# Two score banks and three banks for turned rows; both shared experts split in a row by GpSimd in the last pair

## The reference, cut to what matters

```python
qh = (layernorm(x) @ Wq) by heads; kh, vh = (ctx @ Wk), (ctx @ Wv) by heads
attn = softmax(qh @ kh.T * HEAD_DIM ** -0.5)
x = x + tanh(g_xattn) * ((attn @ vh) @ Wo + bo)
h = layernorm(x)
gates = softmax(h @ router_w); the best two of 14, weights normed to 1
ffn(e) = silu((h * rsqrt(mean(h * h)) * rms_w[e]) @ w1[e]) @ w2[e]
x = x + tanh(g_ffn) * (sum of the two routed ffn, weighted, + both shared ffn)
```

## Time and profile before

| | |
|---|---|
| median of 3 runs | 1499.19 us (1499.08 to 1499.24) |
| profiled execution, own time | 1498.68 us |
| its span, first to last instruction | 1497.0 us, mean granted clock 0.995 |
| busy: TensorE matmuls | 1441.7 us (96%) |
| busy: VectorE | 1086.8 us (73%) |
| busy: ScalarE | 958.3 us (64%) |
| busy: GpSimd | 440.7 us (29%) |
| chain that ended last | TensorE 78%, VectorE 10%, issue 5%, ScalarE 5% |
| pairs 1 to 14 | about 92 to 984 us |
| last pair's steps and the end of the attention | about 984 to 1066 us |

### The profile page before, as it was taken

One profiled execution on the slowest core, in us unless ns is written; L12 is line 12 of the kernel. 1 busy time (PEld: TensorE's weight loads), 2 busy tenths in 40 slices (PEclk: granted clock), 3 DMA queues, 4 the chain that ended last, 5 costly groups with the idle time before them and its releaser, 6 DMA issues.

```text
span 1497.0 us, 32793 instructions
## 1 busy us (share of the span) xinstructions
PE 1441.7 (96%) x9774; PEld 1344.9 (90%) x9774; DVE 1086.8 (73%) x2626; ACT 958.3 (64%) x2413; POOL 440.7 (29%) x676
## 2 busy tenths in 40 slices
PE   6999999999999999999999999998899999999998
PEld 6899999999999999999999999997689988888888
DVE  4778788887878878778787888878668634444448
ACT  4777777777777777777777776775363335455452
POOL 1013132331313313133231323324300135555520
PEclk9999999999999999999999999999999999999999
DMA  4011311212121130311213211141022256653235
GB/s 122 6 30 36 112 73 47 76 49 105 47 80 71 54 104 15 113 71 47 85 40 109 75 47 72 53 153 64 27 99 113 74 180 222 246 203 120 78 121 217
DMA packets 55294, 136.93 MB, mean 91 GB/s; under 512 B 10480, under 2 KB 38144, under 8 KB 51648
## 3 DMA queue, kind: packets, MB, share of 16 engines
q1 hardware_dynamic: 48608, 118.01, 22.7%
q0 software_dynamic: 6624, 18.13, 3.8%
HBM read 86.69 MB, written 49.43 MB: 91 GB/s over the span
## 4 chain that ended last, share of the span: by engine, by line
PE 78%; DVE 10%; issue 5%; ACT 5%; DMA 0%; ACTq 0%; DVEq 0%; POOL 0%; SPq 0%; POOLq 0%
PE bank L531 14%; PE bank L530 14%; PE bank L532 14%; PE bank L588 8%; PE bank L1590 6%; PE bank L933 5%; PE bank L925 5%; PE bank L1610 4%; DVE pT_lo L753 3%; PE bank L1614 2%; PE bank L1600 2%; DVE nmax L770 2%; ACT prob L678 1%; ACT L717 1%; ACT pT_hi L689 1%
## 5 line engine op out<-in xcount | busy, mean ns | idle before, releaser
L678 ACT ACTIVATE prob<-bank,nmax 128x375 f32<-128x375 f32 x448 | 258.7, 577 | 189.1 <-DVE nmax L770 187.2
L770 DVE TENSOR_REDUCE nmax<-bank 128x1 f32<-128x375 f32 x448 | 241.1, 538 | 48.4 <-PE bank L532 47.8
L753 DVE TENSOR_TENSOR pT_lo<-bank,pT_hi 125x384 fp32r<-125x384 f32 x448 | 246.0, 549 | 32.5 <-ACT pT_hi L689 30.7
L588 PE MATMUL bank<-keep_ident,prob 128*125 128x128 f32 x1344 | 225.4, 276 | 25.2 <-DVE pT_lo L753 22.9
L588 PEld LDWEIGHTS bank<-keep_ident,prob 128*125 128x125 f32 x1344 | 198.6, 187 | 45.8 <-DVE pT_lo L753 20.9
L689 ACT CAST pT_hi<-bank 125x384 fp32r<-125x384 f32 x448 | 212.6, 475 | 2.5 <-PE bank L588 2.4
L530 PE MATMUL bank<-attend_wvo_hi,zT_hi 128*112 128x256 f32 x512 | 169.5, 331 | 0.0
L530 PE MATMUL bank<-pT_hi,kv_hi 125*128 125x448 f32 x384 | 152.7, 398 | 6.1 <-DVE zT_lo L753 6.1
L530 PE MATMUL bank<-attend_kvT_hi,qp_hi 128*128 128x376 f32 x448 | 150.3, 335 | 0.2 <-DVE attend_kvT_lo L753 0.2
L531 PE MATMUL bank<-attend_kvT_hi,qp_lo 128*128 128x376 f32 x448 | 150.1, 335 | 0.0
L532 PE MATMUL bank<-attend_kvT_lo,qp_hi 128*128 128x376 f32 x448 | 149.0, 333 | 0.0
(11 more groups left out here) (234 smaller groups left out, 3729.3 us busy)
## 6 DMA issues: line engine op xcount, KB each, us to landing
w_split<-we_split SPq DMA_DIRECT2D x14, 2048.0 KB, 6.8
keep_weights<-w_split SPq DMA_DIRECT2D x14, 2048.0 KB
we_in<-in_w SPq DMA_DIRECT2D x28, 512.0 KB, 5.8
keep_y_all<-y_rows SPq DMA_DIRECT2D x14, 512.0 KB, 9.7
kv_in<-in_ctx SPq DMA_DIRECT2D x32, 187.5 KB
h_rows<-hrow SPq DMA_DIRECT2D x32, 112.4 KB, 2.1
keep_h_in<-h_rows SPq DMA_DIRECT2D x7, 514.0 KB, 8.3
x_in<-in_x SPq DMA_DIRECT2D x16, 224.0 KB, 2.8
```

The source lines that it names most:

```text
L588: last = nc.tensor.transpose(T[s % 2][0:MP, c * P:(c + 1) * P], prob[:, s % NB, c * MP:(c + 1) * MP], ident[:])
L678: nc.scalar.activation(prob[:, s % NB, :], score_bank(s)[:, 0:M], ACT.Exp, bias=nmax[:, s % NB:s % NB + 1], accum_out=psum_[:, s % NB:s % ...
L753: return nc.vector.tensor_tensor(dst, src, hi.bitcast(F32), ALU.subtract)
L770: nc.vector.tensor_reduce(nmax[:, s % NB:s % NB + 1], score_bank(s)[:, 0:M], AX, ALU.max, negate=True).then_inc(max_ready, 1)
```

## The change

The score banks become two, banks 0 and 1, alternating by step; the T banks become three, banks 2 to 4, by step modulo 3, but tile 27 takes the second (so tile 27 and tile 1 of the next pair have the wait of two banks). The scores of tile g wait for the exp of tile g-2 in every step; the turn of tile g waits for `pT_lo` of tile g-3 (of g-2 for tiles 1 and 27). In the last pair GpSimd does the root of batch 29 and `add_bias` ahead of `scale_shared`, then splits both shared experts, then does the roots of batches 30 and 31. At the end ScalarE's roots of batch 30 stand behind `ctx_sums(7)` and the high parts of group 1, and VectorE's `ln2_apply` of batch 30 behind the low parts of group 1 and group 0's logits. No instruction is added or left out.

```diff
--- before.py
+++ after.py
@@ -250,8 +250,8 @@
         we_landed, we_step, we_stored, rms_landed = sem("we_landed"), sem("we_step"), sem("we_stored"), sem("rms_all_landed")
         WE_STEPS = 7
 
-        S = banks[0:3]
-        T = banks[3:5]
+        S = banks[0:2]
+        T = banks[2:5]
         Z, O, SIDE = banks[5], banks[6], banks[7]
         ident = sb["ident"]
 
@@ -305,7 +305,11 @@
 
         def score_bank(s):
 
-            return S[1 if s == STEPS - 1 else s % 3]
+            return S[s % 2]
+
+        def turn_bank_of(s):
+
+            return T[1 if s == STEPS - 1 else s % 3]
 
         def units_of(t):
 
@@ -514,14 +518,14 @@
             split_context(p, 0)
             add_bias(p, 0)
             split_context(p, 1)
-            sb["scale_shared"](pool)
             ln2_root(2 * p - 1)
             add_bias(p, 1)
+            sb["scale_shared"](pool)
             pool.wait_ge(side_done, job_index(p, Q[7]) + 1)
             sb["split_shared"](pool, 0)
+            sb["split_shared"](pool, 1)
             ln2_root(2 * p)
             ln2_root(2 * p + 1)
-            sb["split_shared"](pool, 1)
 
 
         def tensor(pe):
@@ -571,7 +575,7 @@
                 if j == 0:
                     pe.wait_ge(side_lo, kv_job(p, b) + 1)
 
-                need(pe, exp_done, g - 1 if s in (1, STEPS - 1) else g - 2)
+                need(pe, exp_done, g - 1)
                 rows = slice(j * P, (j + 1) * P)
                 three(score_bank(s)[:, 0:MW], [qp[q][:, b, rows] for q in ("hi", "lo")],
                       [kvT[q][:, b, :] for q in ("hi", "lo")], True, True).then_inc(scores_done, 1)
@@ -583,9 +587,9 @@
                     pe.wait_ge(norm_act, STEPS // 2 * p + s // 2 + 1)
                 else:
                     pe.wait_ge(norm_dve, STEPS // 2 * p + s // 2 + 1)
-                need(pe, pT_lo, g - 1)
+                need(pe, pT_lo, g - 1 if s in (1, STEPS - 1) else g - 2)
                 for c in range(MC):
-                    last = nc.tensor.transpose(T[s % 2][0:MP, c * P:(c + 1) * P], prob[:, s % NB, c * MP:(c + 1) * MP],
+                    last = nc.tensor.transpose(turn_bank_of(s)[0:MP, c * P:(c + 1) * P], prob[:, s % NB, c * MP:(c + 1) * MP],
                                                ident[:])
                 last.then_inc(pT_done, 1)
 
@@ -686,7 +690,7 @@
                 g = steps(p, s)
                 act.wait_ge(pT_done, g + 1)
                 need(act, z_done, 8 * p + (P * (s - 6) - 1) // QUAD + 1)
-                nc.scalar.copy(pT["hi"][:, :, ring_place(s)], T[s % 2][0:MP, 0:MC * P].rearrange("p (c n) -> p c n", c=MC)
+                nc.scalar.copy(pT["hi"][:, :, ring_place(s)], turn_bank_of(s)[0:MP, 0:MC * P].rearrange("p (c n) -> p c n", c=MC)
                                ).then_inc(pT_hi, 1)
 
             def ctx_sums(p, qd):
@@ -739,9 +743,9 @@
                 turned(last, STEPS - s)
             ctx_sums(last, 6)
             sb["rows_hi"](act, 0)
-            ln2_roots(B - 2)
             ctx_sums(last, 7)
             sb["rows_hi"](act, 1)
+            ln2_roots(B - 2)
             act.wait_ge(x2_ready, B)
             sb["rows_hi"](act, 2)
             ln2_roots(B - 1)
@@ -781,7 +785,7 @@
 
             def turned(p, s):
                 dve.wait_ge(pT_hi, steps(p, s) + 1)
-                low(pT["lo"][:, :, ring_place(s)], T[s % 2][0:MP, 0:MC * P].rearrange("p (c n) -> p c n", c=MC),
+                low(pT["lo"][:, :, ring_place(s)], turn_bank_of(s)[0:MP, 0:MC * P].rearrange("p (c n) -> p c n", c=MC),
                     pT["hi"][:, :, ring_place(s)]).then_inc(pT_lo, 1)
 
             def ctx_sums(p, qd):
@@ -877,9 +881,9 @@
             sb["split_router"](dve)
             sb["rows_lo"](dve, 0)
             ctx_sums(last, 7)
-            ln2_apply(last, 0)
             sb["rows_lo"](dve, 1)
             sb["copy_logits"](dve, 0)
+            ln2_apply(last, 0)
             ln2_add(last, 1)
             ln2_stats(last, 1)
             ln2_aggregate(last, 1)
```

## The result

| | median | range | ratio to before, 95% interval |
|---|---|---|---|
| before | 1499.22 us (4 runs) | 1499.08 to 1499.53 | |
| after | 1479.04 us (4 runs) | 1478.16 to 1479.70 | 0.9867, 0.9854 to 0.9879 |

The change makes the kernel 20.2 us, or 1.3%, faster; 1480.0 was forecast. The profiled execution took 1478.16 us, with a span of 1476.4, which is 20.6 less than before. Lines of the kernel moved by 4: L588 is now L592, L530 to L532 are L534 to L536, L753 is L757, L779 is L783, L829 and L830 are L833 and L834, L1043 and L1046 are L1047 and L1050.

What follows compares the result with a forecast made beforehand. TensorE was taken to be delayed by turns waiting for `pT_lo` and by two long GpSimd holds of VectorE. Terms a to g sum to -19.1: 1498.68 becomes 1479.6, plus 0.5 gives 1480.0 us; range 1474 to 1491.

Steps and rivals of the forecast that it cites:

- b: Two score banks: exp waits cost nothing in the loop (step 22: 0.67 us cover, 0.60 used); pair 0 wins, -0.5.
- a: Three T banks, pairs 1 to 14: turns in steps 1, 15, 21 less late, 0.85 us a pair, -11.9.
- c: Last pair, steps 0 to 15: 0.35 us won in step 1, about 0.75 in step 15, -1.1.
- d: Last pair, steps 18 and 19: VectorE's 5.37 us hold under the first shared expert's split goes, -7.3 (5.0 to 7.3).
- f: Last pair, both splits' new place: 2.5 L779 arrivals held, mean 2.4 us each, +6.0 (nothing to 15.8).
- e: Last norm, L829 and L830: their hold under the second shared expert's split goes, -4.5 us (3 to 4.8).
- g: Order at the end, batch 30's roots and apply later: batch 31's ln2_add may wait briefly, +0.2 us (0 to 1).
- the first rival: Under the splits, VectorE waits only for the GpSimd instruction in hand: f is 2, total 1476 us; chance 0.2.
- The splits hold VectorE for their whole length: Last pair: the 5.37 us case doubled, f near 15.8, total 1490 us; chance 0.12.
- The waits in the loop only move: Loop: VectorE limits steps 10 to 22, only step 1's 0.35 us comes, a is 4.9, total 1487; chance 0.13.
- The slower case: Loop's L779 held over two subtracts: 2.4 us more lost in each of 14 pairs, total about 1512; chance 0.05.
- The bank change does nothing: New exp waits eat the turns' gain, splits take back what d and e give: 1497 to 1501 us; chance 0.05.

Runs made afterwards that it cites:

- banks and pauses: Kernel after with the old order everywhere, and each cast and subtract of the shared experts' splits waiting for the one before it: 1476.98 us.
- The pauses: Kernel before, GpSimd's order kept, but each cast and subtract of a shared expert's split waits until the one before is complete: 1488.35 us, ratio 0.9920.

## Why the prediction was right, and where it was not

The stages by TensorE's timelines. The kernel after, in order: the last pair's first scores, those of steps 18, 20 and 27, the turn of group 0, the turns that follow a group apart, and the first product of the hidden layer.

```profile
973.74 0.33 PE L534 MATMUL bank<-attend_kvT_hi,qp_hi 128*128 128x376 f32 x1
...
1012.73 0.33 PE L534 MATMUL bank<-attend_kvT_hi,qp_hi 128*128 128x376 f32 x1
...
1017.08 0.33 PE L534 MATMUL bank<-attend_kvT_hi,qp_hi 128*128 128x376 f32 x1
...
1031.91 0.34 PE L534 MATMUL bank<-attend_kvT_hi,qp_hi 128*128 128x376 f32 x1
...
1039.38 1.03 PE L1098 MATMUL bank<-keep_ident,keep_h_in 128*128 128x128 f32 x8
...
1055.20 1.09 PE L1098 MATMUL bank<-keep_ident,keep_h_in 128*128 128x128 f32 x8
...
1057.95 1.09 PE L1098 MATMUL bank<-keep_ident,keep_h_in 128*128 128x128 f32 x8
...
1063.39 0.50 PE L929 MATMUL bank<-keep_hT_hi,keep_w1s_hi 128*128 128x512 f32 x1
```

The same distances in the kernel before, by its own starts:

| stretch | before | after | difference | forecast |
|---|---|---|---|---|
| start to pair 1 | 92.28 | 92.70 | +0.4 | b: -0.5 |
| pairs 1 to 14 | 891.81 | 881.04 | -10.8 | a: -11.9 |
| last pair, steps 0 to 17 | 40.31 | 38.99 | -1.3 | c: -1.1 |
| steps 18 and 19 | 10.92 | 4.35 | -6.6 | d: -7.3 |
| steps 20 to 26, to group 0's turn | 19.74 | 22.30 | +2.6 | f: +6.0 |
| group 0's turn to the hidden layer | 28.89 | 24.01 | -4.9 | e: -4.5, g: +0.2 |
| the rest | 413.00 | 413.04 | 0.0 | 0 |
| sum | | | -20.6 | -19.1 |

That the sum came within 1.0 us of the median is in part luck: a, b and d together gave 2.7 us less than forecast, and f cost 3.4 us less.

**a, right in kind, 1.1 too large.** The wait in step 1 moved behind the turn and steps 15 and 21 are free, as forecast. A pair gained 0.77 us where 0.85 was taken and 0.95 was the sum of the three. By the lengths of the steps, the same in all 14 pairs within 0.04 us, step 1 gained 0.25 where 0.35 was forecast: `sums` start 0.69 us after VectorE begins the subtract that they wait for (598.59), where the turn had started 0.61 us after it (604.32 before); why, no run shows. Step 15 gained 0.32, as forecast. Steps 21 and 22 together gained 0.18 where 0.30 was forecast, and that is the place that b named: "The 0.67 just holds the 0.60". It didn't. The scores of step 22 wait for exp 20 and are 0.21 us late. The forecast priced this at nothing, or 0.1 if the cover goes, and named waiting scores as a sign of being wrong; on this point it was. The wait isn't tried alone; two score banks without the earlier turns don't show it.

The 1.48 us a pair that TensorE idles were not all that could be won. With the table load moved, a pair lasts 62.10 us, 1.60 less than before: the idle leaves out part of a late start, as the prediction itself says in step 15, 0.30 late without a row of idle.

**b, wrong in sign, by 0.9.** In pair 0 the scores wait 1.16 us for an exp. Two score banks alone make pair 0 0.5 us longer (57.06); with the earlier turns it is 56.73, so they give back 0.3 and not more than the price. The other 0.2 of the +0.4 lies ahead of pair 0.

**c, d and e, right in the main.** Both long holds are gone, and with the first its slow clock. e, with g, gave 4.9 us, so the 0.4 us that it kept for a free L829 and L830 cost nothing. d fell 0.7 short of its 7.3. Half of that is the unit: it took steps 18 and 19 for two ordinary steps, 3.62 us, but with the `prob` scaling in them free (0.42 us; GpSimd's order alone, banks and pauses) they last 3.97. The other half, 0.38, is in step 18, where `sums` stands idle for `zT_lo`, which VectorE makes behind an L783 that took 0.79 us under the scaling of the weights (L1039). TensorE's timeline of the kernel after, in step 18 and behind step 27, then VectorE's and GpSimd's:

```profile
1014.21 0.44 PE L534 MATMUL bank<-pT_hi,kv_hi 125*128 125x448 f32 x1 [0.48 <-DVE zT_lo L757]
...
1035.52 0.59 PE L592 MATMUL bank<-keep_ident,prob 128*125 128x128 f32 x3 [0.95 <-DVE prob L783]
```

```profile
1012.75 0.79 DVE L783 TENSOR_SCALAR prob<-prob,prob_inv 128x375 f32<-128x375 f32 x1
...
1014.98 1.10 DVE L833 TENSOR_TENSOR hrow<-rs 112x1 f32<-112x1 f32 x1
1016.01 1.95 DVE L834 TENSOR_SCALAR hrow<-x,mv,rs 112x256 f32<-112x256 f32 x1
...
1029.47 1.55 DVE L783 TENSOR_SCALAR prob<-prob,prob_inv 128x375 f32<-128x375 f32 x1
...
1034.07 1.40 DVE L783 TENSOR_SCALAR prob<-prob,prob_inv 128x375 f32<-128x375 f32 x1
...
1053.72 0.16 DVE L833 TENSOR_TENSOR hrow<-rs 112x1 f32<-112x1 f32 x1 [0.79 <-POOL rs L475]
```

```profile
1014.95 2.85 POOL L1041 TENSOR_SCALAR keep_w_in<-keep_w_in,keep_tanh_g 128x1024 f32<-128x1024 f32 x1
...
1028.41 2.39 POOL L1050 TENSOR_TENSOR keep_w2s_lo<-keep_w_in,keep_w2s_hi 128x1024 fp32r<-128x1024 f32 x1
...
1032.87 2.38 POOL L1050 TENSOR_TENSOR keep_w1s_lo<-keep_w_in,keep_w1s_hi 128x1024 fp32r<-128x1024 f32 x1
```

The last norm's L833 takes 0.16 us where it took 1.94.

**f is the term that was mis-sized: +2.6 against +6.0**, and only 1.7 of the 2.6 lies where the splits hold VectorE. The other 0.8 is in steps 20 to 22, behind L834, which the second weights' scaling (L1041) holds to 1017.96; there TensorE's scores wait 0.17 us for an exp and `sums` 0.34 us for `pT_lo`. The forecast put 2.4 us on each arrival, a mean that contains the hold of 5.37. Three arrivals fell under the splits, at 1025.50 (0.71 us), 1029.47 and 1034.07. On VectorE they cost 0.3, 1.1 and 1.0 us beyond a free 0.42, together 2.4, and each ended within 0.25 us of the end of the GpSimd instruction it met. On TensorE the first cost nothing (steps 23 to 25 last as long as before), the second 0.9 us in step 26 and the third 0.8 between step 27 and group 0's turn. That is the first rival's mechanism, and in this place it was right: its f was 2. The place was as forecast: the splits run from 1023.97 to 1037.7, where "1022 to 1036" stood, and three arrivals fell in where 2.5 were taken.

The Trainium skill (SBUF — State Buffer, Who interferes with whom) says that whoever issues first gets the shared port pair for the whole instruction and that the other is blocked for that time. The traces agree where the splits have pauses (0.97 and 1.44 us, over at the end of a cast and of a subtract), and for the splits in the new place. They disagree where the split runs without pauses in the old place: 5.37, 5.78 and 6.56 us span three or four instructions.

**The rivals.** "The splits hold VectorE for their whole length" fell: under them VectorE's longest operation was 1.55 us. "The waits in the loop only move" fell: pairs gained 0.77, not 0.35. The slower case fell: L783 in the loop is at most 1.60 us, as before. "The bank change does nothing" fell with the run that had the banks alone, -12.5.

**g was nothing**, as its own run shows. **Where the end's gain comes from** was told only half: the forecast took the new place to be what helps. The pauses give the same gain in the old place (-10.7 against -9.4), and with the banks 1476.98 us against 1479.04, so what costs is the unbroken split meeting VectorE there. What stays open is why an unbroken series of eight in the new place let VectorE in after each instruction, and one of four in the old place didn't. The pauses changed nothing in the new place, so they don't settle it. The point of arrival is a rival that no run tests. Under splits without pauses, the `prob` scalings that were held over several instructions met a cast at most 0.48 us after its start (0.08 in the run with only the banks, 0.48 before). Those that met a cast in the new place came at least 0.55 us after its start (1025.50 in the kernel after), and each was let in behind it. So the new place may have helped only because the arrivals fell later into the casts there.

## What to carry to other kernels

When a bank's wait is lifted, look at what is queued right behind the waiting instruction: if it wants the same signal, at most the waiting instruction's own length is won (0.25 us in step 1, where 1.18 were idle), and the cause lies one engine further back (here a table load ahead of a cast, worth 12 us for a move of two lines). Before the place of large GpSimd operations in a row beside VectorE operations that read SBUF is tuned, try a wait on each one's completion ahead of the next: here it took 10.7 us off the kernel before for some 0.4 us of GpSimd a split. Price a hold by the rows of the same kind and keep an outlier like 5.37 out of the mean: it is a case of its own.

## What the runs showed of the hardware that was not expected

- A VectorE operation that meets an unbroken series on GpSimd can be held over several of its instructions: 5.37 us (a cast and two subtracts), 5.78 us (the same) and 6.56 us (two casts and two subtracts, for one number a row). With gaps of 0.12 to 0.14 us between the instructions none was held more than 0.25 us past the end of the one it met.
- A hold can also end before the GpSimd instruction does: with only the end changed, L830 starts at 1025.83, 0.12 us into a scaling (L1037, 2.95 us), and is through after 1.94 us, 0.9 before the scaling ends. In the kernel after, L834 met the same scaling later and was held to its end.
- TensorE's granted clock was 0.72 on average between 1024 and 1036 us before, a stretch with 5.07 us of idle in it, so part of that time was at the lower of its two levels, 1.2 GHz instead of 2.4; without the idle it was 1.00 there. The first work behind the idle, up to the next turn and its three transposes, took 4.42 us, and 2.43 in the kernel after (1014.21 to 1016.64), so the slow clock cost 2.0 us. The two ends of it in TensorE's timeline of the kernel before:

```profile
1030.47 0.71 PE L530 MATMUL bank<-pT_hi,kv_hi 125*128 125x448 f32 x1 [5.07 <-DVE zT_lo L753]
...
1034.89 0.36 PE L530 MATMUL bank<-attend_wvo_hi,zT_hi 128*112 128x256 f32 x1
```

- An activation table load takes 1.28 us of ScalarE each time, and without an explicit request for the table that serves both, logarithm and exp in turn each load their own: six loads a pair in place of one.
